# Latent and rotary attention: the causal mask is added by VectorE instead of TensorE, and a head's reciprocals are taken in one instruction

## What is computed

```
scores = jnp.einsum('bshd,bthd->bhst', qf, kf) * SCALE
mask = jnp.tril(jnp.ones((s, s), bool))
scores = jnp.where(mask[None, None], scores, jnp.finfo(scores.dtype).min)
p = jax.nn.softmax(scores, axis=-1)
out = jnp.einsum('bhst,bthd->bshd', p, v).reshape(b, s, H * DV)
```

## Time and profile before

| what | value |
|---|---|
| median of three runs | 6489.69 us |
| the profiled execution's own time | 6483.94 us |
| its span, first to last instruction | 6482.1 us |
| TensorE busy | 5360.2 us (83% of the span) |
| VectorE busy | 3759.5 us (58%) |
| ScalarE busy | 3136.4 us (48%) |
| GpSimd busy | 1195.5 us (18%) |
| latent attention's four causal phases | within 4006 to 4575 us, with the projections between them |
| rotary attention's four causal phases | within 4847 to 5345 us, likewise |
| DMA in either | about 1% of the engines' time |

### The profile page before, as it was taken

The page is one execution under the profiler, slowest core; times in us unless marked ns, Lnnn a source line. Parts: engine busy times, 40 slices in busy tenths (PEclk is TensorE's granted clock), DMA queues, the critical chain, the costliest instruction groups (busy, mean ns, idle before and its releaser), DMA issues. The chain is left out here.

```text
span 6482.1 us, 91750 instructions
## 1 busy us (share of the span) xinstructions
PE 5360.2 (83%) x30798; PEld 3975.0 (61%) x30798; DVE 3759.5 (58%) x7849; ACT 3136.4 (48%) x9493; POOL 1195.5 (18%) x1216
## 2 busy tenths in 40 slices
PE   4899989999899999999979997888867773577769
PEld 2678777778777777877765555555544442333335
DVE  3666766666666666667653234555345555666661
ACT  1566666666666666666641113444225554333321
POOL 1222222222222222222220001111000000222210
PEclk7999999999999999999989998999979886788879
DMA  1000000000000000000010001000000000000000
GB/s 37 14 21 17 17 17 17 16 19 19 18 16 17 16 17 21 17 16 17 16 44 1 1 10 57 1 1 1 16 19 1 1 1 8 17 1 0 0 20 13
DMA packets 47176, 93.40 MB, mean 14 GB/s; under 512 B 11984, under 2 KB 19184, under 8 KB 45712
## 3 DMA queue, kind: packets, MB, share of 16 engines
q1 hardware_dynamic: 46736, 88.07, 4.6%
HBM read 85.67 MB, written 2.38 MB: 14 GB/s over the span
## 5 line engine op out<-in xcount | busy, mean ns | idle before, releaser
L857 ACT ACTIVATE dh_pb<-bank 64x128 f32<-64x128 f32 x3072 | 831.3, 271 | 272.0 <-PE bank L631 238.7
L645 PE MATMUL bank<-dh_cw,dh_pb 128*128 128x128 f32 x5120 | 701.6, 281 | 112.9 <-ACT dh_pb L857 111.4
L645 PEld LDWEIGHTS bank<-dh_cw,dh_pb 128*128 128x128 f32 x5120 | 635.7, 193 | 191.0 <-ACT dh_pb L857 164.3
L995 DVE SCALAR_TENSOR_TENSOR dh_kq<-bank,dh_conv_kq,dh_kq 128x511 f32<-128x511 f32 (+2 forms) x408 | 305.3, 748 | 184.0 <-ACT dh_kq L814 172.8
L863 ACT ACTIVATE dh_cw<-bank 128x256 f32<-128x256 f32 x640 | 245.0, 385 | 254.9 <-PE bank L645 247.6
L582 PE MATMUL bank<-hT,dh_w_kq 128*128 128x512 f32 x544 | 276.3, 632 | 82.6 <-DVE dh_kq L995 75.2
L995 DVE SCALAR_TENSOR_TENSOR dh_v<-bank,dh_conv_v,dh_v 128x511 f32<-128x511 f32 (+2 forms) x384 | 284.0, 747 | 91.3 <-ACT dh_v L814 82.3
L1669 PE MATMUL bank<-moe_h_split,moe_w 128*128 x1200 | 279.5, 383 | 22.6 <-PEq L88 15.0
L1930 POOL TENSOR_TENSOR blk_att_e<-blk_att_e,blk_att_block_share 128x128 f32<-128x128 f32 (+3 forms) x256 | 185.3, 724 | 475.7 <-DVE blk_att_block_share L1903 475.7
L594 PE MATMUL bank<-dh_w_vz,hT 128*128 128x256 f32 x1024 | 245.5, 383 | 22.0 <-ACT dh_zs L825 22.0
L262 POOL TENSOR_TENSOR ln_rstd<-ln_var_eps,nhalf 128x16 f32<-128x16 f32 x8 | 23.2, 2903 | 1266.7 <-DVE ln_var_eps L252 1266.7
(11 more groups left out here) (399 smaller groups left out, 13262.3 us busy)
## 6 DMA issues: line engine op xcount, KB each, us to landing
dh_rates<-delta_rates SPq DMA_DIRECT2D x130, 256.0 KB, 3.5
dh_w_vz<-in_L_wvz SPq DMA_DIRECT2D x17, 512.0 KB, 3.3
mod_w<-in_L_wmod SPq DMA_DIRECT2D x4, 1536.0 KB, 6.4
dh_w_kq<-in_L_wkq SPq DMA_DIRECT2D x18, 256.0 KB, 2.6
dh_wo<-in_L_wo SPq DMA_DIRECT2D x16, 256.0 KB, 4.2
moe_w<-in_L_w13T SPq DMA_DIRECT2D x1, 3200.0 KB, 16.0
x_res<-in_x SPq DMA_DIRECT2D x1, 2048.0 KB, 8.2
mla_wA<-in_L_wA SPq DMA_DIRECT2D x1, 2048.0 KB, 8.5
```

Of the source, the lines that this page charges most:

```text
L645: last = pe.matmul(square(j)[:, b, :, :], pb[j][:, b, :], src[:, :, b, :], start=True, stop=True)
L857: last = act.activation(out[half, :, o, half], src[halves[o], :, half], ACT.Copy)
L995: dve.scalar_tensor_tensor(y, pj_bank(n)[:, 0:S - i], taps(n)[:, TAPS - 1 - i:TAPS - i], y, ALU.mult, ALU.add).then_inc(s["v_cs" if i < TA ...
```

## The change

TensorE's scores(h, t) is one float32 matmul and no mask for causal attention. VectorE gets `corner(h, t)`: it adds the float32 mask to the last 128 columns of bank t, in place in PSUM. maximum(h, t) waits for it. The four reciprocals of a head are one instruction, `total_head`, on four columns; it waits for the exponents of all four tiles of the head. VectorE's order for a head is now: corner(h, 0), maximum(h, 0), corner(h, 1), total_head(h - 1), scale_row(h - 1, 0), scale_row(h - 1, 1), maximum(h, 1), corner(h, 2), scale_row(h - 1, 2), maximum(h, 2), corner(h, 3), scale_row(h - 1, 3), maximum(h, 3). Block attention keeps its instructions and their order.

```diff
@@ scores
-                    pe.matmul(bank[t][:, 0:keys(t)], qT(head)[:, t * P:(t + 1) * P], kT(head)[:, 0:keys(t)],
-                              start=True, stop=False, skip_group_check=True)
-                    pe.matmul(bank[t][:, t * P:(t + 1) * P], k.ident_h[:, :], mask[:, :], start=False, stop=True,
-                              skip_group_check=True).then_inc(scored, 1)
+                    last = pe.matmul(bank[t][:, 0:keys(t)], qT(head)[:, t * P:(t + 1) * P], kT(head)[:, 0:keys(t)],
+                                     start=True, stop=not blocks, skip_group_check=True)
+                    if blocks:
+                        last = pe.matmul(bank[t][:, t * P:(t + 1) * P], k.ident_h[:, :], k.blockneg_h[:, :], start=False,
+                                         stop=True, skip_group_check=True)
+                    last.then_inc(scored, 1)
@@ VectorE
+                def corner(h, t):
+                    n = NC * h + t
+                    dve.wait_ge(scored, n + 1)
+                    diagonal = bank[t][:, t * P:(t + 1) * P]
+                    dve.tensor_tensor(diagonal, diagonal, k.causal[:, :], ALU.add).then_inc(cornered, 1)
+
+                def total_head(h):
+                    dve.wait_ge(expd, NC * (h + 1))
+                    dve.reciprocal(rl[:, h % 2, :], l[:, h % 2, :]).then_inc(rec, 1)
+
+                def scale_row(h, t):
+                    dve.wait_ge(rec, h + 1)
+                    dve.tensor_scalar(row(h, t), row(h, t), rl[:, h % 2, t:t + 1], None, ALU.mult).then_inc(scaled, 1)
+
                 def maximum(h, t):
                     n = NC * h + t
                     dve.wait_ge(scored, n + 1)
                     if not blocks:
+                        dve.wait_ge(cornered, n + 1)
                         after(dve, expd, n - 2 * NC + 1)
...
+                    if new: corner(h, 0)
+                    if new: maximum(h, 0)
+                    if new: corner(h, 1)
+                    if old: total_head(h - 1)
+                    for t in range(NC):
+                        if old: scale_row(h - 1, t)
+                        if new and t > 0: maximum(h, t)
+                        if new and 1 <= t < NC - 1: corner(h, t + 1)
```

More of the change, by code:

```diff
@@ L1800, in attend @@
         bmax, bsum, rec, share = (ph.sem(n) for n in ("bmax", "bsum", "rec", "share"))
+        cornered = ph.sem("cornered")
         keys = lambda t: (t + 1) * P
         inner = lambda ap: ap.rearrange("p (j n) -> p j n", n=BLOCK)
-        mask = k.blockneg_h if blocks else k.causal_h
         bank = k.bank
@@ L1885, in total @@
                     dve.wait_ge(expd, n + 1)
[L1886 to L1889, removed]
+                    dve.tensor_reduce(bz[:, n % 2, 0:nb], inner(row(h, t)), AX_X, ALU.add).then_inc(bsum, 1)
                 def inverse(h, t):
@@ L1901, in scale @@
                     dve.wait_ge(rec, n + 1)
+                    dve.tensor_tensor(bc[:, 1, n % 2, 0:nb], bc[:, 0, n % 2, 0:nb], blocks[:, t, 0:nb], ALU.mult)\
+                        .then_inc(share, 1)
+                for h in range(heads + 1):
+                    new, old = h < heads, h > 0
                     if blocks:
[L1903 to L1913, removed]
+                        for t in range(NC):
+                            if old: total(h - 1, t)
                             if old: inverse(h - 1, t)
@@ L1917, in _ @@
                             if new: less_maximum(h, t)
-                        else:
-                            if old: scale(h - 1, t)
-                            if new: maximum(h, t)
+                        continue
+                    if new: corner(h, 0)
+                    if new: maximum(h, 0)
+                    if new: corner(h, 1)
+                    if old: total_head(h - 1)
+                    for t in range(NC):
+                        if old: scale_row(h - 1, t)
+                        if new and t > 0: maximum(h, t)
+                        if new and 1 <= t < NC - 1: corner(h, t + 1)
             if blocks:
```

## The result

| what | before | after |
|---|---|---|
| median of the runs | 6488.83 us (4 runs, 6486.56 to 6490.51) | 6527.20 us (4 runs, 6525.29 to 6532.97) |
| ratio to before, 95% interval | | 1.0061 (1.0043 to 1.0078) |
| the profiled execution: its time, its span | 6483.94 us, 6482.1 us | 6526.60 us, 6524.8 us |
| TensorE busy | 5360.2 us | 5361.3 us |
| VectorE busy | 3759.5 us | 3817.8 us |

The change costs 0.6%, 38 us. I forecast 6505 with a range up to 6526, so it came out just above the range, with the sign that I gave the larger chance.

What follows compares the result with a forecast made beforehand. VectorE was taken to bound the even head after the change; per phase 0.3 + 0.34 + 6 x 0.17 + 0.2 = 1.86, over 8 phases 15 us, on a median of 6489.69: 6505 us, range 6480 to 6526.

Steps and rivals of the forecast that it cites:

- the sign that I gave the larger chance: Whole kernel: slower, chance 0.52, against 0.43 for the same and 0.05 for faster.
- The price of the add: VectorE's 128-column add in PSUM: 0.29 us long, next instruction 0.20 after its start.
- What bounds the pair: Causal pair of heads: VectorE bounds the even head E, without a gap; TensorE idles some 0.3 around turn(G, 0).
- the masks' saving: TensorE's removed mask matmuls: at most 0.32 us per head, 41 us for 128 heads; gone at turn(G, 0), 4.15 against 4.08.
- the sum for the causal waits: Eight causal phases: 1.86 us more per phase from filling, six pairs and tail, 15 us in all.
- the pairs: Six pairs of heads per causal phase: each takes 10.65 us, 0.17 more.
- the fillings: First two heads of each causal phase: 0.3 us more for the first, 0.34 for the second.
- the tails: End of each causal phase, last head's scales waiting for its last exponent: 0.2 us more, bounded above by about 1.3.
- a cost of nothing for block attention: Block attention, behind the causal phases: no term in the sum, which covers only the 8 phases.
- the clock only as a rival in the pairs: TensorE's clock in the causal pairs falls to a mean of 0.83: 86 us more, 6575; chance 0.04.
- the cheap add: Rival, VectorE's add costs what the reciprocal does: at most 0.24 us gained a pair, 6478 to 6490; chance 0.17.
- the add that holds VectorE for its whole length: Rival, no overlap behind each add: 0.51 us more a pair, 34 us in all, 6524; chance 0.13.

Runs made afterwards that it cites:

- experiment 9: Changed kernel with added matmuls in block attention, and VectorE's corner(h, 3) moved behind scale_row(h - 1, 3): 6481.61 us, ratio 0.9990; a causal pair took 10.74.
- experiment 2: Changed kernel with four separate reciprocals, each ahead of its scale, so only the adds and VectorE's new order remain: 6544.03 us, ratio 1.0087.
- experiment 4: Changed kernel with a pause (one VectorE memset of 1600 columns, and a barrier) ahead of block attention's loop: 6511.17 us, ratio 1.0034.
- experiments 5 and 6: Kernel before, then changed kernel, each with unused 512-column matmuls in block attention's TensorE waits: 6446.07 us (0.9936) and 6472.61 us (0.9966).
- all four kernels with a pause: VectorE memset ahead of block attention: 1600 columns, kernel before 6492.79 us, changed 6511.17 us; 3200 columns, before 6490.47 us, changed 6507.25 us.
- experiment 1: Changed kernel with the mask back on TensorE and no adds, keeping the joint reciprocal and VectorE's new order: 6491.69 us, ratio 1.0009.

## Why the prediction was wrong

**Right, point by point.** The price of the add: 0.29 and 0.20 forecast, 0.29 and 0.19 to 0.21 measured. What bounds the pair: VectorE in head E's stretch without a gap, TensorE waiting there for the scale for 0.30, the masks' saving gone at turn(G, 0); experiment 9 confirms it, and experiment 2, where more work on VectorE in that stretch made the pair longer.

**Right by luck: the sum for the causal waits.** 15 forecast, 14.2 measured, but out of other shares: I had 8.2 for the pairs, 5.1 for the fillings and 1.6 for the tails, and 5.4, 3.3 and 3.7 were measured, with 1.8 between the phases. A pair costs 0.10 more, not 0.17. The first start that needs an add's result comes 0.06 later than I took, and against that weigh_pair follows exponent(E, 3) by less than I carried over, since the old distance was TensorE's queue. The tail's 0.2 holds where the clock stayed up (0.19 to 0.21); the rest of the 3.7 is clock. So the parts that I had walked measure about 10 us, not 15, and a lower clock fills the sum up. The latent phases, which I had not walked, show a last pair of 10.79 after five of 10.60.

**Wrong: a cost of nothing for block attention.** The sum covers 8 causal phases and has no term for what follows them, since no instruction there changes. It took 23.7 us more, over half of the whole. What the runs showed in place of that nothing: its pairs hold waits for GpSimd of 1.5 and 1.8 us, TensorE's clock falls to 1.2 GHz in most pairs, and how much work the low clock covers, in the pairs and in the stretches between the sequences, depends on when the sequence starts against it. The kernel before happened to start so that a sequence takes 167.2; the kernel after takes 173.2 to 174.1; with a memset in between it takes 167.3 again (experiment 4), and with the waits filled the pairs of the two kernels are equal and 7 us are left outside them (experiments 5 and 6).

**Wrong: the clock only as a rival in the pairs.** I asked if it would fall in the stretch where TensorE is 9 of 10 busy. It did not: 1.00 there, as the row below shows. It fell where TensorE was already waiting, in the tails of the phases, and took at least 7.4 us of the 21.6 in these two executions. The Trainium skill (TensorE: Matmul & The Clock Gate, HAM oscillation) has the clock go back to its lower level where waits recur; by that rule the places to check were the tails and block attention, whose granted clock of 0.66 stood in rows 1. The trace agrees, with waits of 1.40 in a tail and 1.82 in block attention; the section's example has longer waits, for DMAs.

Busy time by stretch after, 10 us within a rotary phase:

```profile
4877.00:4887.00 10.00, 9.26 (x51) 5.27 (x52) 7.39 (x25) 6.72 (x23) 0.00 (x0) 1.00 0.01 2
```

The rivals: the cheap add is out by its 0.29; the add that holds VectorE for its whole length is out by the next start at 0.20, although its total of 6524 was nearest to what was measured. That number came close for a reason that does not hold. The Trainium skill's rule behind it (VectorE: DVE Perf Modes, The DRAIN you can't avoid) was quoted without its limit: the same section says that an operation that is not held starts earlier. The trace agrees with that: instructions with no need of the result start 0.20 into an add of 0.29.

**Open.** Why the kernel after keeps 174 us per sequence while all four kernels with a pause, and experiments 1 and 2, drift to 167 is not explained by the runs; they show that the start decides, not by what rule. That the low clock in the causal tails comes from the wait of 1.40 for the joint reciprocal is read from the traces and not tested. It fits experiments 1 and 2: with the joint reciprocal alone none of the eight last weigh_pairs ran at full clock throughout, with separate reciprocals five did. But the causal code of before has only one to three at full clock in its four profiled executions, so this fit proves little.

## What to carry to other kernels

Before work moves from a busy engine to one with slack, add up the receiving engine's own stretch between the same two events, latencies included: here a third of the time free on average was 0.61 us in the stretch that counted, and four adds used it up. Price a change also in the stages behind it, wherever TensorE waits long enough for its clock to fall: a shift of a few us there cost as much as the edit did in its own stages (23.7 against 21.6). Read the phases themselves and not only the stages around them: in experiment 1 a stage total of 4.4 us hid 16.2 in the phases. And where such waits can't be removed, useless matmuls in them can pay: 16 a sequence bought 0.64% of the whole program.

## What the runs showed that I had not expected

- Unchanged code took 167.2 or 174.1 us per sequence, depending on when it started; a memset of 1600 columns ahead of it made the program 16 us faster.
- An in-place add in PSUM costs VectorE no more than one that writes to SBUF: 0.29 long, 0.20 to the next start, both.
- The reciprocal of four columns takes 0.17 to 0.18 us against 0.15 for one.
- More matmuls made TensorE busy for less time: 118.91 us with 16 more in a sequence, against 119.70.
